# Moving the first tokens' routing and the next row norms in between the last two output additions of the first attention

## What is computed

```python
x = x + tanh(g_xattn[0]) * L0_xattn(layernorm(x), ctx)   # 16 heads of 128, keys from 64 context rows
x = x + tanh(g_ffn[0])   * L0_ffn(layernorm(x))          # mixture: 64 experts, 8 chosen, + shared MLP
x = x + tanh(g_xattn[1]) * L1_xattn(layernorm(x), ctx)   # 16 heads of 16
x = x + tanh(g_ffn[1])   * L1_ffn(layernorm(x))          # 8 experts, 2 chosen, + shared MLP
```

```python
scores = sigmoid(x @ router_weight.T); sc = scores + e_bias
group_scores = top_k(sc.reshape(n, 8, 8), 2)[0].sum(-1)   # best 4 of 8 groups are kept
topk_idx = top_k(masked sc, 8); topk_w = scores / sum * 2.5
```

## Time and profile before

| | |
|---|---|
| median of 3 runs | 1303.04 us (1300.71 to 1304.79) |
| the profiled execution's own time | 1301.03 us |
| its span in the profile | 1299.1 us |
| busy in the span: PE, PEld, DVE, ACT, POOL | 79%, 66%, 56%, 33%, 21% |
| mean granted TensorE clock | 0.839 of full |
| end of the first attention, from norms of group 0 to the last output addition | 341 to 390 us |
| routing loop | 391 to 468 us |

### The profile page before, as it was taken

One profiled execution on the slowest core, in us unless ns is written; L12 is line 12 of the kernel. 1 busy time (PEld: TensorE's weight loads), 2 busy tenths in 40 slices (PEclk: granted clock), 3 DMA queues, 4 the chain that ended last, 5 costly groups with the idle time before them and its releaser, 6 DMA issues. The chain is left out here.

```text
span 1299.1 us, 16804 instructions
## 1 busy us (share of the span) xinstructions
PE 1021.7 (79%) x5531; PEld 853.7 (66%) x5531; DVE 725.6 (56%) x1700; ACT 434.6 (33%) x810; POOL 278.5 (21%) x225
## 2 busy tenths in 40 slices
PE   5989989989874700767677367878889899999998
PEld 3867857768664500656566236464657899989898
DVE  7267667685658887222223478475766644445443
ACT  4555555464633300111111033423253333232331
POOL 0414304223000000788888310100100000000000
PEclk8999999999986755877877667767665999989999
DMA  7004000000000140788887550000000000000000
GB/s 274 4 1 141 1 1 1 1 1 1 1 1 20 40 134 8 170 171 173 183 174 142 125 204 1 2 0 0 0 1 1 1 1 17 1 17 0 17 1 17
DMA packets 58942, 66.42 MB, mean 51 GB/s; under 512 B 5070, under 2 KB 55688, under 8 KB 58120
## 3 DMA queue, kind: packets, MB, share of 16 engines
q1 hardware_dynamic: 45236, 46.45, 11.5%
q0 software_dynamic: 12288, 18.88, 8.3%
q10 hardware_dynamic: 1363, 0.37, 0.1%
HBM read 48.13 MB, written 17.56 MB: 51 GB/s over the span
## 5 line engine op out<-in xcount | busy, mean ns | idle before, releaser
L2034 PE MATMUL bank<-gu_hi,xnT_split 128*128 128x352 f32 x640 | 163.7, 329 | 3.7 <-DVE soft L1232 3.7
L485 POOL TENSOR_TENSOR q_lo<-soft,q_hi 128x512 fp32r<-128x512 f32 x64 | 93.2, 1456 | 236.5 <-ACT soft L1370 236.4
L2034 PEld LDWEIGHTS bank<-gu_hi,xnT_split 128*128 128x128 f32 x640 | 114.3, 191 | 4.6 <-DVE soft L1232 4.0
L506 POOL DMA_INDIRECT acc<-y,dst_now x64 | 102.2, 1596 | 26.0 <-issue 18.9
L496 POOL DMA_INDIRECT xg<-table,src_now x64 | 64.0, 1000 | 203.0 <-DVE src_now L951 183.8
L2034 PE MATMUL bank<-gu_lo,xnT_split 128*128 128x352 f32 x320 | 104.1, 325 | 0.0
L1232 DVE SCALAR_TENSOR_TENSOR soft<-sg,combine_w,bank 128x176 f32<-128x176 f32 x160 | 56.4, 394 | 69.4 <-PE bank L2034 63.8
L724 DVE COPY qT<-bank 128x512 f32<-128x512 f32 x64 | 44.2, 691 | 87.9 <-PE bank L1730 86.8
L1837 PEld LDWEIGHTS bank<-xgT,w_gu 128*88 128x88 f32 x512 | 79.8, 202 | 7.0 <-issue 4.4
L1837 PE MATMUL bank<-xgT,w_gu 128*88 128x128 f32 x512 | 81.6, 328 | 0.7 <-issue 0.7
L971 DVE TENSOR_SCALAR y<-bank,xg 128x256 f32<-128x256 f32 x64 | 28.0, 480 | 96.8 <-PE bank L1850 81.8
(11 more groups left out here) (276 smaller groups left out, 2355.9 us busy)
## 6 DMA issues: line engine op xcount, KB each, us to landing
w_gu<-in_L_ffn_w_gu SPq DMA_DIRECT2D x32, 352.0 KB
w_dn<-in_L_ffn_w_down SPq DMA_DIRECT2D x32, 176.0 KB
acc<-zeros SPq DMA_DIRECT2D x2, 2176.0 KB, 11.3
acc_rows<-acc SPq DMA_DIRECT2D x8, 512.0 KB, 4.9
gu<-in_L_gu SPq DMA_DIRECT2D x1, 3520.0 KB, 13.5
table<-xw SPq DMA_DIRECT2D x4, 640.0 KB
wo<-in_L_xattn_Wo SPq DMA_DIRECT2D x2, 1024.0 KB, 15.2
wq<-in_L_xattn_Wq SPq DMA_DIRECT2D x1, 2048.0 KB, 17.6
```

What stands on the lines that cost most here:

```text
L485: pool.tensor_tensor(q2_lo[:, h % 3, :], q2[h % 2], q2_hi[:, h % 3, :], ALU.subtract).then_inc(q2_split, 1)
L506: pool.indirect_dma_start(acc[e], bass.IndirectOffsetOnAxis(ap=dst_now[:, q, e:e + 1], axis=0), y[:, q, e, :], None, compute_op=ALU.add).t ...
L2034: mm = pe.matmul(b[:, 0:2 * F1], v[:, c, j * P:(j + 1) * P], w[:, c, p, o, :], start=(n == 0), stop=(n == len(terms) - 1))
```

## The change

VectorE no longer waits for outputs 2 and 3 before it raises `done1`; it does not wait for the others' `done1` at all. The first group's route is written out ahead of the loop, whose copies for groups 1 and 2 stay a loop. In it the addition of output 2 stands behind `normed(1)`, and the addition of output 3 behind the routing of group 0. TensorE takes over the wait for output 3's addition, ahead of the first product that overwrites the bank. The routing's temporaries move from `soft` to the place of `acc_rows`, which is free from the end of the query projections until the expert stage is over. ScalarE's and SyncE's waits for `done1` stay.

```diff
-        sigs = soft[:, 3, 512:1024].rearrange("p (b n) -> p b n", b=2)
-        keys2 = soft[:, 2, 0:512].rearrange("p (j h e) -> p j h e", j=G, h=2)
-        part = [soft[:, n // 4, (n % 4) * 256:(n % 4 + 1) * 256] for n in range(16)]
...
         acc_rows = sb("acc_rows", [P, 2, NA, G, DIM], scope=rows)
+        route_t = acc_rows[:].rearrange("p b n j d -> p (b n) (j d)")
+        sigs = route_t[:, 3, 512:1024].rearrange("p (b n) -> p b n", b=2)
+        keys2 = route_t[:, 2, 0:512].rearrange("p (j h e) -> p j h e", j=G, h=2)
+        part = [route_t[:, n // 4, (n % 4) * 256:(n % 4 + 1) * 256] for n in range(16)]
...
             divide(G - 1, T_LAST + 2 * (G - 1))
-            residual(NG - 1, G - 2, one_bank=True)
-            residual(NG - 1, G - 1, one_bank=True)
-            dve.wait_ge(o_read, 2 + NT)
             dve.drain().then_inc(done1["dve"], 1)
...
             dve.wait_ge(zeroed, 16 * NA)
-            for e in done1.values():
-                dve.wait_ge(e, 1)
...
-                dve.wait_ge(t_ring.free, T2 + TRF + TR * i)
+                dve.wait_ge(t_ring.free, T2 - T_HEADS + TRF if i is first_group else T2 + TRF + TR * i)
                 if not last:
                     normed(i + 1, EPS0)
+                if i is first_group:
+                    residual(NG - 1, G - 2, one_bank=True)
...
                                          op1=ALU.mult).then_inc(rows_ready, 1)
+                if i is first_group:
+                    residual(NG - 1, G - 1, one_bank=True)
+                    dve.wait_ge(o_read, 2 + NT)
                 for j in range(G):
                     residual(NG + i, j, i, 2)
...
-            with dve.Fori(0, NG - 1) as i:
+            first_group = 0
+            route(first_group, False)
+            with dve.Fori(1, NG - 1) as i:
                 route(i, False)
...
                 pe.wait_ge(q_ring.free, Q2 + QR * (i + 1))
+                if i is first_group:
+                    pe.wait_ge(o_read, 2 + NT)
                 for j in range(G):
...
-            with pe.Fori(0, NG - 1) as i:
+            first_group = 0
+            route(first_group, False)
+            with pe.Fori(1, NG - 1) as i:
                 route(i, False)
```

## The result

The changed kernel takes 1294.09 us (median of 6 runs, 1292.78 to 1296.56) against 1302.70 for the kernel before (6 runs, 1300.52 to 1304.79). The ratio is 0.9937 with a 95% interval of 0.9926 to 0.9948: 8.2 us less, between 6.8 and 9.6 (the ratio is that of the means; the medians differ by 8.6 us).

A forecast was written before the change was run, and what follows sets the result against it. VectorE was taken to bound the route loop, idling 9.1 us ahead of it. The first shared addition 4.56 us earlier, less 0.32 for the loop's entry, gave 4.2: 1303.04 to 1298.8 us, range 1295.0 to 1301.7.

The forecast's parts named there:

- the bound of each side: VectorE bounds the route loop (busy 18.40 of 20.65 us); ahead of the loop VectorE waits for TensorE's outputs.
- the idle stretch that was filled: VectorE after the last softmax: waits of 4.26 and 4.85 us for outputs 2 and 3, 9.1 us idle.
- VectorE's chain: After the last softmax: norms, addition 2, routing, addition 3 done at 399.62; alone it would gain 9.5 us.
- the bound goes to TensorE for this step: First route step: VectorE idles about 5 us from 399.62 until the first shared addition at 404.60.
- the table load: ScalarE behind output 3: load starts 0.36 us after it, takes 1.28 us, and now the tokens wait for it.
- Rival D: Slower: code transfers stall at three new places, 2.9 us each, 8.7 us in all; 1307.5 us; chance 0.05.
- Output 3 at 5.41 us: TensorE's output 3, after 2.03 us of idling, runs partly at half clock: 5.41 us, ending at 392.67.
- the 2.07 row: Profile row of before: a TensorE output that came after 2.07 us of idling and took 5.41 us.
- From the logits to the first shared product 8.31 us: First route step on TensorE: duration taken over from the profile of before, 408.39 - 400.08.
- rival A: Output 3 keeps full clock, 3.72 us: gain 5.9, 1297.1 us; logits and shared products too add 3.1; chance 0.23.
- the hand-over to VectorE: From the first shared product on TensorE to the first shared addition on VectorE: 0.77 us.
- The loop's entry: Now behind the written-out first route: costs between nothing and 0.32 us; 0.32 taken off the gain.

The follow-up runs named there:

- the filled kernel before: The kernel before with 15 matmuls without use behind TensorE's drain, where it waits for normed tokens; 1305.16 us (one run).
- the shortest seam here: Changed kernel without ScalarE's waits, banks swapped, group 1 statistics ahead of addition of output 0, matmuls without use on TensorE; 1294.23 us, ratio 0.9937.

## Why the prediction was wrong

**Right:** the bound of each side, the idle stretch that was filled, the order of events, and VectorE's chain. From the last softmax, norms 0.78 us later (forecast 0.95), addition 2 at 6.43 (6.59), output 3 at 7.05 (7.13), addition 3 begun at 18.52 (19.01). That the bound goes to TensorE for this step is right too (hole of 2.12 us, 5 forecast), and the table load is in the path, as the run without ScalarE's waits shows (0.6 us from the end of output 3 to the logits, not the load's whole 1.28). Loads, stores and expert stage moved with the seam. Rival D is answered: no stall at any new place.

**Wrong:** two terms of TensorE's chain, both for the clock. Measured from the last softmax, the first shared addition was forecast at 24.47 us (404.60 - 380.13) and came at 21.12, 3.35 earlier:

- *Output 3 at 5.41 us* ("its idle time is nearest to the 2.07 row"). It took 3.72, or 3.69 where it did wait 2.06 us for the addition. The term was mis-sized by 1.7 us. The row chosen did not bear the weight: in the changed kernel output 0, after the same 2.07 us, took 3.72. In the attention of the last group, over the twelve profiles, 14 outputs came right after 2.06 to 2.19 us of idling; 10 took 3.69 to 3.72 us and 4 took 5.38 or 5.41. Idle time of this length is followed now by the one, now by the other, and the quick output was the likelier. That the forecast held it for the slower one rested on the one profile there was.
- *From the logits to the first shared product 8.31 us*, taken from a step that TensorE enters after 7.66 us of idling. Here it enters from work: 6.97 us (393.05 to 400.02), so the term was 1.3 us too long, of which the logits give 1.2. The run with idle time filled in the kernel before shows the cause by itself: 5.31 us there (399.13 to 404.44), in the old order. How much comes of it varies: 5.31 at best, 6.97 in both profiles of the changed kernel, and logits of 3.54 us with addition 2 ahead of the norms. I had this as an extra under rival A, where it belonged in the sum: the step's neighbours had changed, so its durations could not be carried over.
- The rest is small: output 3 to logits 2.66 us instead of 2.85, drain and waits 0.33 instead of 0.53, the hand-over to VectorE 0.72 instead of 0.77.

Of the 8.42 us gained at the second step's start, 3.35 are this, 4.56 the forecast's own figure ahead of the loop's entry, and 0.51 come from an earlier last softmax in the profiled execution (379.62 against 380.13), which is no effect of the change. The loop's entry takes nothing off: from the first shared addition to the next statistics it is 3.11 us before and after. Rival A is what happened, with 1.3 of the 3.1 us of its further gain; the seam then accounts for 7.9 of the 8.2 us.

One reading of the forecast was too round: the step of the kernel before was not without a hole. VectorE waits 0.48 us in it for a shared product (at 410.56), so that stage already hung on TensorE in part.

The Trainium skill's rule in "TensorE: Matmul & The Clock Gate", Part 1, that activity releases the clock and that the point of change moves from run to run, agrees with these runs: output 2 took 5.3, 5.41 and 6.3 to 6.4 us in different profiles, and 3.72 where matmuls without use stood ahead of it. That the slower output was the likelier one by it, as the forecast concluded, did not come out (4 of 14). It was also read for one output only, and not for what follows it.

A sum over one profile also had an average hidden in it. In the old order a slow output 2 or 3 lies in VectorE's path; in the new one a part is covered. The profile of before held a middling output 2, so the gain from that could not be read in it; the 30.08 us of the filled kernel before shows its size, 1 us.

## What to carry to other kernels

When work is moved into an engine's idle time, cost the stages behind it at the clock they will then find, not at the one of today's trace: a step that TensorE used to enter cold may be entered warm. One profile shows one draw of that clock, so give both levels a price. A late link on a chain matters only if it ends last there; moving the addition forward made the kernel slower. Measure from a point ahead of everything that moved: the shortest seam here looked 5 us shorter than the changed kernel's and was 1.3 us shorter once the delay ahead of it and the next step were counted in.

## What was not expected of the hardware

TensorE's logits (8 products, 16 records of 128x64) take 3.67 us at half clock and 1.99 at full, though only 64 columns move per matmul: a stage of small matmuls gains nearly the whole factor too. And an idle stretch of 2.07 us led to an output of 5.41 us in the profile of before and of 3.72 in that of the changed kernel, while 3.63 us led to 5.38.
